# A four-stage attention and FFN kernel: in its last stage, half of the roundings by GpSimd, and the head in another order

## What is computed

```python
def act_quant(x):
    scale = 127.0 / jnp.clip(jnp.max(jnp.abs(x), axis=-1, keepdims=True), 1e-05)
    return jnp.clip(jnp.round(x * scale), -128, 127) / scale
def weight_quant(w):
    scale = 1.0 / jnp.clip(jnp.mean(jnp.abs(w)), 1e-05)
    return jnp.clip(jnp.round(w * scale), -1, 1) / scale
def bit_linear(x, w):                      # the straight-through form has this value
    return jnp.einsum('bsd,hd->bsh', act_quant(x), weight_quant(w))
h = bit_linear(layernorm(x), w1)                     # 256 -> 1024
h = depthwise_conv1d(h.transpose(0, 2, 1), conv_w, conv_b).transpose(0, 2, 1)   # 3 taps over s
x = x + bit_linear(silu(h), w2)                      # 1024 -> 256
```

## Time and profile before

| | us |
|---|---|
| runs (3), median | 666.99 (666.47 to 669.52) |
| the profiled execution | 666.55 |
| its span, first to last instruction | 664.8 |
| last stage, from 583.2 to the end of the span | 81.6 |
| granted clock of TensorE, mean of the span (1 is 2.4 GHz) | 0.925 |

### The profile page before, as it was taken

One profiled execution on the slowest core, in us unless ns is written; L12 is line 12 of the kernel. 1 busy time (PEld: TensorE's weight loads), 2 busy tenths in 40 slices (PEclk: granted clock), 3 DMA queues, 4 the chain that ended last, 5 costly groups with the idle time before them and its releaser, 6 DMA issues. The chain is left out here.

```text
span 664.8 us, 14715 instructions
## 1 busy us (share of the span) xinstructions
PE 551.0 (83%) x5314; PEld 469.4 (71%) x5314; DVE 366.6 (55%) x1117; ACT 369.6 (56%) x872; POOL 149.1 (22%) x230
## 2 busy tenths in 40 slices
PE   2899999999858149999999995779999999746636
PEld 2687787888646149999999985668878887545525
DVE  3777666666634611131222106598776767457795
ACT  2778787787733003332332223488978878565563
POOL 2123344434044141111112006503022222100000
PEclk9999999999876659999999997799999999967788
DMA  6322211011039675666565404400111110000001
GB/s 158 133 71 71 71 56 52 15 47 49 2 100 349 237 293 159 184 204 212 191 191 196 151 16 135 124 2 12 38 49 48 49 48 2 1 2 1 0 1 55
DMA packets 33497, 62.79 MB, mean 94 GB/s; under 512 B 4130, under 2 KB 24435, under 8 KB 33300
## 3 DMA queue, kind: packets, MB, share of 16 engines
q1 hardware_dynamic: 28756, 47.05, 21.5%
q0 software_dynamic: 2928, 10.75, 5.6%
q10 hardware_dynamic: 1744, 4.06, 1.6%
HBM read 51.11 MB, written 10.75 MB: 93 GB/s over the span
## 5 line engine op out<-in xcount | busy, mean ns | idle before, releaser
L1296 ACT ACTIVATE ex_h_t<-ex_h,b_e 128x128 f32<-128x128 f32 x168 | 47.9, 368 | 127.6 <-PE ex_h L1552 127.6
L893 PE MATMUL a_ring<-ident,a_e 112*125 112x112 f32 x768 | 100.3, 280 | 6.6 <-ACT a_e L478 6.5
L893 PEld LDWEIGHTS a_ring<-ident,a_e 112*125 112x125 f32 x768 | 88.8, 189 | 23.8 <-issue 12.8
L486 ACT ACTIVATE a_et<-a_ring 125x448 f32<-125x448 f32 x128 | 62.8, 541 | 46.3 <-PE a_ring L893 46.3
L1552 PE MATMUL ex_h<-ex_xg_t,w_s 128*128 128x128 f32 x672 | 79.8, 278 | 0.0
L662 DVE CUSTOM_DVE_ANT_0 a_e<-a_s,mask_sb 112x375 f32<-112x375 f32 x128 | 65.5, 544 | 24.3 <-issue 13.2
L655 DVE TENSOR_REDUCE a_mx<-a_s 112x2 f32<-112x750 f32 x64 | 59.7, 933 | 34.2 <-PE a_s L884 34.2
L1552 PEld LDWEIGHTS ex_h<-ex_xg_t,w_s 128*128 128x128 f32 x672 | 78.2, 195 | 0.1
L1571 PE MATMUL ex_y<-w_all,ex_h_t 128*128 x336 | 75.9, 379 | 0.0
L478 ACT ACTIVATE a_e<-a_e,a_shift 112x375 f32<-112x375 f32 x128 | 68.9, 600 | 4.1 <-DVE a_shift L667 3.0
L1571 PEld LDWEIGHTS ex_y<-w_all,ex_h_t 128*128 128x128 f32 x336 | 62.3, 190 | 7.6
(11 more groups left out here) (279 smaller groups left out, 804.6 us busy)
## 6 DMA issues: line engine op xcount, KB each, us to landing
w_s<-in_L_ffn_W SPq DMA_DIRECT2D x18, 1024.0 KB, 5.4
w_all<-in_L_ffn_W SPq DMA_DIRECT2D x8, 1024.0 KB, 12.1
ct_dram<-a_ct SPq DMA_DIRECT2D x8, 752.0 KB, 4.4
a_ct<-ct_dram POOLq DMA_DIRECT2D x8, 752.0 KB
w_s<-in_L_ffn_W ACTq DMA_DIRECT2D x3, 1024.0 KB, 11.7
a_ctx<-in_ctx SPq DMA_DIRECT2D x8, 375.0 KB
y_slots<-ex_y_sb SPq DMA_DIRECT2D x21, 128.0 KB, 1.7
w_ud<-in_L_ffn_w SPq DMA_DIRECT2D x2, 1024.0 KB, 7.7
```

The lines of the kernel that those rows point to most:

```text
L486: a.activation(et[:, t % 2, kc], bank("et", t, kc)[0:KP, 0:4 * S], ACT.Copy)\
L893: last = nc.tensor.transpose(bank("et", t, kc)[0:KP, r * S:(r + 1) * S], es[:, t % 2, r, kc * KP:(kc + 1) * KP], ident[0:S, 0:S])
L1296: last = a.activation(h_t[:, i % 2, f], hb[i % 2][:, f * 128:(f + 1) * 128], ACT.Gelu, bias=b1_e[:, i % 2, f:f + 1])
```

## The change

- `rounded(0, j)` leaves VectorE. ScalarE copies the first half's spread scales from PSUM to a new SBUF tile `spread_sb`, behind its silu of chunk 5 of the second half. GpSimd then does two fp32 operations for each chunk, `hp = hs * spread_sb` and `hp = hp + NR` in place, with two buffers; ScalarE's activation with bias `-NR` takes NR off again and writes bf16. GpSimd's chunk j waits for ScalarE's chunk j - 2.
- VectorE keeps `rounded(1, j)`, without the first half's before it.
- ScalarE rounds chunks 0 and 1 of the first half ahead of `diagonal(1)`, the other six behind it (before: 0 to 4 ahead, 5 to 7 behind).
- The head: the root is made by GpSimd (add epsilon, power -0.5), 4 batches at a time; the normalizing is VectorE's (`normal(half)`); ScalarE loads one table, at the very start, and copies all 8 weights in a row; VectorE does moments of both halves, `normal(0)`, `quantized(0)`, `dequantized(0)`, `normal(1)`, `lower(0)`, `quantized(1)`, where `lower(0)` stood behind `quantized(1)` before.

The diff without the lines that declare tiles and semaphores:

```diff
@@ -1665,6 +1672,27 @@
                             sp.dma_start(out.rearrange("b s d -> s b d")[:, bs], x_sb[:, bs]).then_inc(stored, 16)
                         sp.wait_ge(stored, 32)
 
+                    @block.gpsimd
+                    def _(pool):
+                        g = nc.gpsimd
+                        g.memset(power[:], -0.5).then_inc(power_out, 1)
+                        g.memset(less_nr[:], -NR).then_inc(power_out, 1)
+                        pool.wait_ge(power_out, 2)
+                        for half in range(2):
+                            bs = slice(HB * half, HB * half + HB)
+                            pool.wait_ge(mv_out, HB * half + HB)
+                            g.tensor_scalar(var[:, bs], mv[:, bs, 1], LN_EPS, None, ALU.add).then_inc(var_out, 1)
+                            pool.wait_ge(var_out, half + 1)
+                            g.tensor_tensor(rstd[:, bs], var[:, bs], power[:], ALU.pow).then_inc(rstd_out, 1)
+
+                        pool.wait_ge(r_sb, 1)
+                        for j in range(FC):
+                            if j >= 2:
+                                pool.wait_ge(hq_out, j - 1)
+                            g.tensor_tensor(hp[:, j % 2], hs[:, j, columns(0)], spread_sb[:], ALU.mult).then_inc(hp_raw, 1)
+                            pool.wait_ge(hp_raw, j + 1)
+                            g.tensor_scalar(hp[:, j % 2], hp[:, j % 2], NR, None, ALU.add).then_inc(hp_out, 1)
+
                     @block.scalar
                     def _(act):
                         a = nc.scalar
@@ -1677,16 +1705,8 @@
                                 dst = wd_t[:, 2 * (q - 4):2 * (q - 3)].rearrange("p c d -> p (c d)")
                             a.activation(dst, wide[q][:], ACT.Copy).then_inc(wt_out, 1)
 
-                        for q in range(4):
-                            weight(q)
-                        act.wait_ge(var_out, 1)
-                        a.activation(std[:], mv[:, :, 1], ACT.Sqrt).then_inc(std_out, 1)
                         a.activation(tick[:], ones[0:1, 0:1], ACT.Silu)
-                        act.wait_ge(shift_out, 2)
-                        for b in range(B):
-                            a.activation(xn[:, b], x_sb[:, b], ACT.Identity, bias=shift_x[:, b:b + 1],
-                                         scale=rstd[:, b:b + 1]).then_inc(xn_out, 1)
-                        for q in range(4, 8):
+                        for q in range(8):
                             weight(q)
                         act.wait_ge(c_in, 32)
 
@@ -1711,8 +1731,12 @@
 
                         def rounded(half, j):
                             n = FC * half + j
-                            act.wait_ge(hr_out, n + 1)
-                            a.activation(hq[:, j, columns(half)], hr[:, n % 2], ACT.Copy).then_inc(hq_out, 1)
+                            if half == 0:
+                                act.wait_ge(hp_out, j + 1)
+                                a.activation(hq[:, j, columns(0)], hp[:, j % 2], ACT.Identity, bias=less_nr[:, 0:1])                                    .then_inc(hq_out, 1)
+                            else:
+                                act.wait_ge(hr_out, j + 1)
+                                a.activation(hq[:, j, columns(1)], hr[:, j % 2], ACT.Copy).then_inc(hq_out, 1)
 
                         def diagonal(half):
                             act.wait_ge(a_out, half + 1)
@@ -1729,12 +1753,14 @@
                                 silu(half, j)
                                 if half and j == 3:
                                     diagonal(0)
-                                if half and j >= 6:
-                                    rounded(0, j - 6)
-                        for j in range(2, 5):
-                            rounded(0, j)
+                                if half and j == 5:
+                                    act.wait_ge(r_ps, 1)
+                                    a.activation(spread_sb[:], pr[0][:, 0:HALF], ACT.Copy).then_inc(r_sb, 1)
+                                if half and j == 7:
+                                    rounded(0, 0)
+                        rounded(0, 1)
                         diagonal(1)
-                        for j in range(5, FC):
+                        for j in range(2, FC):
                             rounded(0, j)
                         for j in range(FC):
                             rounded(1, j)
@@ -1743,17 +1769,19 @@
                     def _(dve):
                         link = link_dve(dve)
                         v = nc.vector
-                        for b in range(B):
-                            v.bn_stats(stats[:, b], x_sb[:, b]).then_inc(stats_out, 1)
-                        for b in range(B):
-                            dve.wait_ge(stats_out, b + 1)
-                            v.bn_aggr(mv[:, b], stats[:, b]).then_inc(stats_out, 1)
-                        dve.wait_ge(stats_out, 2 * B)
-                        v.tensor_scalar(mv[:, :, 1], mv[:, :, 1], LN_EPS, None, ALU.add).then_inc(var_out, 1)
-                        dve.wait_ge(std_out, 1)
-                        v.reciprocal(rstd[:], std[:]).then_inc(shift_out, 1)
-                        dve.wait_ge(shift_out, 1)
-                        v.scalar_tensor_tensor(shift_x[:], mv[:, :, 0], -1.0, rstd[:], ALU.mult, ALU.mult).then_inc(shift_out, 1)
+
+                        def moments(half):
+                            for b in batches(half):
+                                v.bn_stats(stats[:, b], x_sb[:, b]).then_inc(stats_out, 1)
+                            for b in batches(half):
+                                dve.wait_ge(stats_out, b + 1)
+                                v.bn_aggr(mv[:, b], stats[:, b]).then_inc(mv_out, 1)
+
+                        def normal(half):
+                            dve.wait_ge(rstd_out, half + 1)
+                            for b in batches(half):
+                                v.tensor_scalar(xn[:, b], x_sb[:, b], mv[:, b, 0:1], rstd[:, b:b + 1], ALU.subtract,
+                                                ALU.mult).then_inc(xn_out, 1)
 
                         def scales(which, half, wide_am, am_of):
                             bs = slice(HB * half, HB * half + HB)
@@ -1806,7 +1834,7 @@
                         def rounded(half, j):
                             n = FC * half + j
                             dve.wait_ge(r_ps, half + 1)
-                            if n >= 2:
+                            if j >= 2:
                                 dve.wait_ge(hq_out, n - 1)
                             v.tensor_tensor(hr[:, n % 2], hs[:, j, columns(half)], pr[half][:, 0:HALF], ALU.mult).then_inc(hr_out, 1)
 
@@ -1815,10 +1843,14 @@
                             v.scalar_tensor_tensor(x_sb[:, b, :], pd[b // HB][b % HB][0:S, 0:D], dq[:, 1, b:b + 1],
                                                    x_sb[:, b, :], ALU.mult, ALU.add).then_inc(d_out, 1)
 
+                        moments(0)
+                        moments(1)
+                        normal(0)
                         quantized(0)
                         dequantized(0)
+                        normal(1)
+                        lower(0)
                         quantized(1)
-                        lower(0)
                         dve.wait_ge(c_in, 32)
                         for j in range(FC):
                             taps(0, j)
@@ -1835,13 +1867,9 @@
                                 highest(1, j - 2)
                             if j == 2:
                                 token_scale(0)
-                            if j >= 5:
-                                rounded(0, j - 5)
                         for j in range(FC - 2, FC):
                             highest(1, j)
                         token_scale(1)
-                        for j in range(3, FC):
-                            rounded(0, j)
                         for j in range(FC):
                             rounded(1, j)
                             if j in (3, 5):
```

## The result

| | before | after |
|---|---|---|
| median of 7 runs each, us | 666.99 (665.93 to 669.52) | 673.47 (671.62 to 675.01) |
| ratio after / before, 95% interval | 1 | 1.0079 (1.006 to 1.0099) |
| the profiled execution, us | 666.55 | 674.07 |
| its span | 664.8 | 672.4 |
| last stage, from its first moments on | 81.3 | 85.8 |

The changed kernel is slower, by 6.5 us between the medians. The prediction said 668.0 with a range up to 671.2, and it gave "slower" a chance of 0.21: it was wrong.

The account below looks back on a forecast made before the run. VectorE was taken to bound the last stage before, GpSimd the turn after the change. Head -4.4, turn +5.2 and TensorE's clock +0.6 sum to +1.4 on 666.55: 668.0 us, range 664.5 to 671.2.

Parts of the forecast that it names:

- the turn's sum: From the second half's loop to `down(0)`: GpSimd's eight pairs at 1.81 us and its stop put `down(0)` 5.2 us later.
- Head: From the stage's first moments to VectorE's first tap: the new order brings the first tap 4.4 us earlier.
- the lean rival: Pair 1.65 us, VectorE not held, TensorE's clock high for the head's transposes (0.8 us less): 664.3 us, chance 0.14.
- that rival: In the head, GpSimd's power holds VectorE too, costing about 0.5 us in `normal(0)`: 668.5 us, chance 0.05.
- Multiplication: At the turn, GpSimd's multiplication of a chunk by the spread scales, 448 columns wide: 1.15 us.
- The hand-over: Between GpSimd's operations in a pair of multiplication and addition: some 0.06 us, within a pair of 1.81 us.
- VectorE held by GpSimd: Behind the last maximum, GpSimd's wide operations hold VectorE's small ones, so the second half's scales come 1.5 us late.
- GpSimd's stop before its fifth pair: At the turn, GpSimd waits about 1.3 us because ScalarE's rounding of the third pair stands behind the late `diagonal(1)`.
- `down(0)`, from the stage's start: Start of TensorE's first `down(0)` product: 654.8 instead of 649.6 us, +5.2, before the head's 4.4 us are taken off.
- Clock: In the tail, TensorE's clock climbs later because it idles some 6 us before `down(0)`: +0.6 us, bounds -0.4 and +1.5.
- the addition is as dear as the multiplication: Rival at the turn: GpSimd's addition costs 1.15 us, a pair 2.36, `down(0)` +8.3 us: 671.1 us, chance 0.18.
- from about 2.2 us: GpSimd's price per pair from which the dear-addition rival decides; below it the end is within 0.5%.

Follow-up runs that it names:

- the two-operation one: Changed kernel with GpSimd adding NR as times 1.0 plus NR in one instruction, instead of a single addition: 667.58 us, ratio 0.9989 against before.
- fillers: Unread transposes put into TensorE's idle stretches at the turn: on the changed kernel 673.52 us (1.0053), on the new head alone 0.9917, on the three-chunk shared kernel 0.9869.

## Why the prediction was wrong

**The step that failed** is one term of the turn's sum: "so 0.6 us at 448; the other end is that it costs what the multiplication costs, 1.15. I take 0.6, because it too reads one tensor". The addition took 1.33 us. Neither end held it: the upper one was taken from the multiplication, as if an operation with one input could not be dearer than one with two. The nearest row was a cast, and a cast reads and writes as much, but it was a row of another operation. The error is 0.7 us a pair, eight times over: 5.7 us in front of `down(0)`, of which the stop before the fifth pair, which then has no room, gives back about 1.3.

By the sum's own terms, against the runs:

- Head: forecast -4.4 us. Measured -5.3 in the changed kernel, -4.6 in the kernels in which the head's eight transposes ran at the low clock (1.75 us instead of 1.02). The path was as described. The 0.7 us between the two are the lean rival's clock term, which came in the changed kernel and the two-operation one and not in eight others with the same head. Normalizing by VectorE beside GpSimd's power took 1.39 us against 1.37: the power, 1.09 us long and all but 0.25 of it beside them, doesn't hold VectorE, and that rival is out.
- Multiplication: forecast 1.15 us, measured 1.13. The hand-over is 2.52 - 1.13 - 1.33 = 0.06 us, as forecast.
- VectorE held by GpSimd: forecast 1.5 us late. In the changed kernel two of the three small operations of that form were stretched, to 0.41 and 0.85 us from 0.17 and 0.23, which makes 0.9 us; in the two-operation kernel one, to 1.06, again 0.9. The mechanism is there, the size was somewhat less. The reciprocal among them was never stretched (0.18 us). In the changed kernel:

```profile
640.39 0.41 DVE L1789 TENSOR_SCALAR bf_am<-bf_am 112x4 f32<-112x4 f32 x1
...
641.05 0.85 DVE L1791 TENSOR_SCALAR bf_dq<-bf_am,wmean 112x4 f32<-112x4 f32 x1
```

- GpSimd's stop before its fifth pair: forecast 1.3 us, 1.27 in the two-operation kernel, 2.60 without the addition, and none in the changed kernel.
- `down(0)`, from the stage's start: forecast 66.40 - 4.4 + 5.2 = 67.2. With the pair that was measured it would be 67.2 + 8 x 0.71 - 1.3 (no stop) - 0.95 (the better head) = 70.6; the changed kernel had 70.31. With the cheap form it was 65.52; the 1.7 us below the forecast are the better head (1.0), eight pairs at 1.75 instead of 1.81 us (0.5), and 0.2 of rest.
- Clock: forecast +0.6 us for the tail, measured +0.5. The clock was at 2.4 GHz 4.6 us after `down(0)` began and before 3.6 us, and half of that 1.0 us is 0.5. So the path was right in the changed kernel; that it hit the number is luck, since the tails of the kernels without fillers lay between 13.90 and 16.12 us, and in the two-operation kernel the tail was 0.4 us shorter than before. The fillers show that the whole low clock is worth 2.2 us in the changed kernel.

With that one term put right the mechanism stands, step by step. The kernel that differs by the cheap form alone gave 667.58 us where the prediction had 668.0, but this closeness is luck: the prediction had +1.4 us against before, and that kernel had -1.2 in its stage and -0.4 in the median (0.9989, up to 1.0005). The 2.6 us between +1.4 and -1.2 are the 1.7 us at `down(0)` and 1.0 in the tail. Of the first, 0.7 is TensorE's clock at the head's transposes, and the second is its clock in the tail, where `down(0)`'s 16 products took 3.29 us against 3.66 before; the prediction had the clock come back later than before.

**The rival that came about** is "the addition is as dear as the multiplication", with 671.1 us and a chance of 0.18. It had `down(0)` at 657.9 - 4.4 in times of before, that is 70.3 us from the stage's start, and 70.31 was measured. That too is luck in part: its pair was 0.16 us too cheap (eight times, 1.3 us) and its head gained 0.95 us less than the real one, which nearly cancels. Its condition was not met either, as the addition is dearer than the multiplication (1.33 against 1.13 us). The stage lost 4.4 us, where that rival had +4.5. The median is 2.4 us above its 671.1 all the same. The profiles put nothing of this into the last stage, and the ratio's interval begins at +4.0 us; where the rest of the median's difference lies is open.

The range was too narrow on the one side where a price had no row of its own. By the prediction's own count a pair decides "from about 2.2 us". The measured pair is 0.3 above that, not on the edge.

## What to carry to other kernels

A price taken from the nearest row must come from the same kind of operation; where there is none, the upper end is not the price of some heavier-looking operation, and an experiment that times the operation alone is cheap. On GpSimd, write the addition of a constant to a wide fp32 tile as times 1.0 plus the constant, in one instruction (0.57 us for 1.33 at 448 columns). When an engine that was idle takes work over from a busy one, compare its whole chain with the time until its result is wanted: with the same head, VectorE alone gave 0.9925 of before, all eight chunks on GpSimd 0.9989 even in the cheap form, and three chunks on GpSimd had `down(0)` a microsecond earlier, which did not show in the time (0.9918) until TensorE's clock was held as well (0.9869).

## What was not expected of the hardware

- GpSimd's fp32 operation of a tensor and a constant, 128 partitions: with a single operation 1.34 us at 448 columns, 0.77 at 224, 0.37 at 64, some 2.5 ns a column. A multiplication with an addition in one instruction: 0.57, 0.38 and 0.24 us. Addition with subtraction: 1.73 us.
- A small VectorE operation of the form TENSOR_SCALAR is held by GpSimd's wide ones to their end (0.17 becomes 1.06 us). A power on 112x4 numbers didn't hold it, and a VectorE reciprocal wasn't held.
- TensorE's clock fell in the second of two pauses (1.63 and 0.77 us), though 3.9 us of work without a break stood just ahead of them; it stayed up where most of the second pause was filled, and through a pause of 2.40 us behind 10.0 us of fillers. And the same new head did its eight transposes in 1.0 us in two profiles, 1.25 in one and 1.67 to 1.76 in the other eight, in kernels that hardly differ up to that point: 0.7 us that a forecast can't place.
